# A conv, state-space and attention block on one Trainium2 core: one product moved to GpSimd, MLP and SiLU steps re-placed in a hand-made schedule

## What is computed

```python
# layer 0, per sample; xn = rmsnorm over channels of x
u, z = in_proj(xn);  u = silu(causal_conv4(u))           # forward; the same on the reversed sequence
B, C, dt = x_proj(u); delta = softplus(dt_proj(dt))
h = exp(delta*A)*h + (delta*u)*B;  y = sum_n h*C + u*D    # 16 states n, two directions d
g = (fwd + bwd) out-projected, y gated by silu(z)
local = sigmoid(depthwise3x3(xn) + dw_b) * xn             # the "local product"
x = x + res_scale * (g*scale_mod + local)
# layer 1, per sample: tokens t, 6 heads of 64, causal
t = t + attention(layernorm(t));  t = t + mlp(layernorm(t))   # mlp: narrow input of 32, 1536 hidden, gelu
```

## Time and profile before

| | us |
|---|---|
| median of 3 runs | 4040.74 (4040.47 to 4043.13) |
| profiled execution, its own time | 4045.01 |
| span of the profiled execution | 4043.1 |
| DVE busy | 3526.4 (87%) |
| PE busy | 3405.5 (84%) |
| POOL busy | 2820.7 (70%) |
| ACT busy | 2593.5 (64%) |

### The profile page before, as it was taken

How to read it: one execution, slowest core, us unless ns; L and a number is a source line. 1 busy time by engine, 2 the same in 40 slices (tenths; PEclk the granted TensorE clock), 3 DMA queues, 4 the chain that set the end, 5 groups by cost and what they waited for, 6 DMA issues and landing times.

```text
span 4043.1 us, 39821 instructions
## 1 busy us (share of the span) xinstructions
PE 3405.5 (84%) x11722; PEld 1723.8 (43%) x11722; DVE 3526.4 (87%) x2678; ACT 2593.5 (64%) x3592; POOL 2820.7 (70%) x1714
## 2 busy tenths in 40 slices
PE   7504499989999898988899889988989889985999
PEld 2101136623474245723366234742457233651473
DVE  6999999999999999999999999999999999999121
ACT  4533567676686767756676756867677666766363
POOL 3889886687866877677866878668776778668000
PEclk8757699988999899988999889988999889997999
DMA  3999897898977998788987989788987889789000
GB/s 103 234 248 240 190 242 181 207 209 207 219 190 188 227 214 202 190 201 198 237 188 199 222 202 216 186 193 224 215 198 194 203 201 232 179 197 221 6 7 16
DMA packets 220548, 770.79 MB, mean 191 GB/s; under 512 B 24908, under 2 KB 40574, under 8 KB 220062
## 3 DMA queue, kind: packets, MB, share of 16 engines
q0 software_dynamic: 113616, 413.71, 52.9%
q1 hardware_dynamic: 106702, 354.32, 26.4%
HBM read 339.60 MB, written 39.85 MB: 94 GB/s over the span
## 4 chain that ended last, share of the span: by engine, by line
PE 43%; DVE 21%; issue 12%; ACT 9%; POOL 8%; DMA 7%; ACTq 0%; DVEq 0%; POOLq 0%
DVE pB L1313 14%; PE pW L710 9%; PE pW L623 9%; DMA y<-hb 6%; PE pW L511 6%; POOL hb L1527 5%; PE pW L588 3%; PE pW L639 3%; PE pW L554 3%; ACT pt L1071 2%; POOL prob L1501 2%; PE pW L785 2%; DVE hb L1322 1%; PE pW L602 1%; PE pW L742 1%
## 5 line engine op out<-in xcount | busy, mean ns | idle before, releaser
L1313 DVE TENSOR_TENSOR_SCAN pB<-pB,hb 128x1024 f32<-128x1024 f32 x768 | 1757.4, 2288 | 64.1 <-ACT pB L889 52.1
L1542 POOL DMA_DIRECT2D y<-hb x765 | 748.9, 979 | 628.0 <-DVE hb L1322 578.3
L1527 POOL TENSOR_TENSOR hb<-du_f,b_row 128x1024 f32<-128x1024 f32 x384 | 1003.3, 2616 | 157.4 <-DMA y<-hb 71.9
L1527 POOL TENSOR_TENSOR hb<-uc_b,b_row 128x1024 f32<-128x1024 f32 x384 | 996.4, 2596 | 75.2 <-DMA y<-hb 62.0
L1322 DVE TENSOR_TENSOR hb<-pB,c_row 128x1024 f32<-128x1024 f32 x768 | 940.5, 1225 | 44.6 <-DVE pB L1313 0.5
L889 ACT ACTIVATE pB<-delta,vec 128x1024 f32<-128x1024 f32 x384 | 429.2, 1118 | 303.2 <-DVE hb L1322 290.3
L889 ACT ACTIVATE pB<-xres,vec 128x1024 f32<-128x1024 f32 x384 | 427.9, 1119 | 214.7 <-DVE hb L1322 213.7
L710 PE MATMUL pW<-area,pt 128*128 128x64 f32 x3456 | 440.1, 282 | 19.2 <-ACT pt L1071 11.5
L710 PEld LDWEIGHTS pW<-area,pt 128*128 128x128 f32 x3456 | 413.1, 196 | 68.9 <-ACT pt L1071 58.8
L1360 DVE TENSOR_REDUCE stat<-pW 128x1 f32<-128x640 f32 (+7 forms) x361 | 258.7, 753 | 162.4 <-PE pW L626 162.4
L530 PE MATMUL pW<-area,xn_area 128*128 128x512 f32 x576 | 260.7, 608 | 31.9 <-DVE area L1418 19.0
(11 more groups left out here) (185 smaller groups left out, 5010.3 us busy)
## 6 DMA issues: line engine op xcount, KB each, us to landing
y<-hb POOLq DMA_DIRECT2D x765, 512.0 KB, 7.7
b_row<-bc_rows SPq DMA_DIRECT2D x256, 512.0 KB, 5.9
c_row<-bc_rows SPq DMA_DIRECT2D x256, 512.0 KB, 5.8
du_f<-in_x SPq DMA_DIRECT2D x8, 1536.0 KB, 13.9
kept_residual<-in_x SPq DMA_DIRECT2D x8, 1536.0 KB, 18.9
xres<-kept_residual SPq DMA_DIRECT2D x8, 1536.0 KB, 14.5
out_x<-xa SPq DMA_DIRECT2D x7, 1536.0 KB, 9.5
kept_residual<-hb POOLq DMA_DIRECT2D x16, 512.0 KB, 5.3
```

Source lines behind the costliest of these rows:

```text
L1313: dve.tensor_tensor_scan(flow(d, buf), flow(d, buf), flow(d, hb[r % NHB][:, :]), 0.0, ALU.mult, ALU.add).then_inc(scan_done, 1)
L1527: pool.tensor_tensor(hb[r % NHB][:, :], du[d][:, k, :], b_row[g % 2][:, :], ALU.mult)\
L1542: pool.dma_start(y[:, k, :], hb[r % NHB][:, :], accum_op=ALU.add).then_inc(y_in[k], 16)
```

## The change

Five things change, in the order of the diff.

1. `mlp_add` moves from slot r+9 to r+10 of each half, and the second half starts at slot 81 instead of 82. `mlp_add` 0 moves from slot 81 to 82, where now also the second half's first GELU lies, behind it; its later GELUs move from 85, 87, 89 to 84, 86, 88; `mlp_out` 1 moves from 90 to 89; `mlp_add` 1 stays in 91.
2. `wo_add` 5 comes behind `next_norm` in slot 66. `next_square` goes from early to late in slot 63, so behind `decay(64)`. `step_silu` joins `SOON`: in slot 17 it now stands ahead of `proj` 2.
3. The local product of group 2 goes to GpSimd: ScalarE multiplies the sigmoid's result by `rs_col` in place (behind `skip`, ahead of slot 0), and GpSimd multiplies by `xnp` inside `keep_local`, which for this group is behind the input of slot 2.
4. At the head the order on ScalarE becomes: taps to 7, narrow copies, tap 8, sigmoid 0, `soft_abs` 0, sigmoid 2, sigmoid 1.
5. The narrow MLP input stays in PSUM (`pS`) from `mlp_scale` on: cast, split, low and fix read it there, and the 32-partition copy of `mlp_fix` (L1404) goes from VectorE to ScalarE.

```diff
-        ("mlp", c * (NFG + 1) + NFG, r + 2 * NFG), ("mlp_out", c, r + 2 * NFG), ("mlp_add", c, r + 2 * NFG + 1)]
+        ("mlp", c * (NFG + 1) + NFG, r + 2 * NFG), ("mlp_out", c, r + 2 * NFG), ("mlp_add", c, r + 2 * NFG + 2)]
...
-    + [("wo_add", t, S1 + (3 if t < 2 else 5)) for t in range(6)]
-    + [("next_square", 0, S1 + 2), ("next_mean", 0, S1 + 2), ("next_rstd", 0, S1 + 4), ("next_norm", 0, S1 + 5)]
+    + [("wo_add", t, S1 + (3 if t < 2 else 5)) for t in range(5)]
+    + [("next_square", 0, S1 + 2), ("next_mean", 0, S1 + 2), ("next_rstd", 0, S1 + 4), ("next_norm", 0, S1 + 5), ("wo_add", 5, S1 + 5)]
...
-       ("mlp_split", 0, S1 + 10), ("mlp_low", 0, S1 + 11), ("mlp_fix", 0, S1 + 11)] + mlp(0, S1 + 11) + mlp(1, S1 + 21), key=lambda x: x[2])
-SOON = [x for x in BEHIND if x[0] == "step_abs"]
+       ("mlp_split", 0, S1 + 10), ("mlp_low", 0, S1 + 11), ("mlp_fix", 0, S1 + 11)] + mlp(0, S1 + 11) + mlp(1, S1 + 20), key=lambda x: x[2])
+SOON = [x for x in BEHIND if x[0] in ("step_silu", "step_abs")]
...
                 if g == 2:
-                    pe.wait_ge(loc_ready, at(KT, b, BRANCH.index(1) + 1))
+                    pe.wait_ge(loc_ready, at(VK, b, VK))
...
-                    act.activation(taps[k], taps[k], ACT.Sigmoid).then_inc(sig_ready, 1)
+                    act.activation(taps[k], taps[k], ACT.Sigmoid).then_inc(sig_ready if k < VK else gate_ready, 1)
...
-                    act.copy(xr_a, xr_rest[:, :]).then_inc(xr_step, 1)
+                    act.copy(xr_a, pS).then_inc(xr_step, 1)
...
-                    act.copy(xr_b, xr_rest[:, :]).then_inc(xr_step, 1)
+                    act.copy(xr_b, pS).then_inc(xr_step, 1)
+                    act.copy(xr_a[3 * KI:4 * KI, :], pS[3 * KI:4 * KI, :]).then_inc(xr_step, 1)
...
-                elif kind == "next_square" and early:
+                elif kind == "next_square" and not early:
...
-                    tap_row_of(b, TAPS[6], 9)
+                    tap_row_of(b, TAPS[6], 8)
+                    narrow_copies(b, 0)
+                    tap_row_of(b, 8, 9)
                     gates(b, 0, 1)
-                    narrow_copies(b, 0)
-                    gates(b, 1, 2)
                     soft_abs(b, 0, 0)
-                    gates(b, 2, 3)
+                    gates(b, 1, 3)
...
+                    act.wait_ge(gate_ready, at(1, b, 1))
+                    act.activation(taps[VK], taps[VK], ACT.Identity, scale=rs_col).then_inc(gate_scaled, 1)
...
-                        dve.tensor_tensor(part, part, pW[:, c, :], ALU.mult).then_inc(xr_scaled, 1)
+                        dve.tensor_tensor(pW[:, c, :], part, pW[:, c, :], ALU.mult).then_inc(xr_scaled, 1)
...
-                    dve.tensor_tensor(xr_rest[:, :], xr_rest[:, :], xr_a, ALU.subtract).then_inc(xr_step, 1)
+                    dve.tensor_tensor(pS, pS, xr_a, ALU.subtract).then_inc(xr_step, 1)
...
-                    dve.tensor_copy(xr_a[3 * KI:4 * KI, :], xr_b[3 * KI:4 * KI, :]).then_inc(xr_step, 1)
-                    dve.tensor_tensor(xr_b[0:KI, :], xr_rest[0:KI, :], xr_b[0:KI, :], ALU.subtract)\
+                    dve.tensor_tensor(xr_b[0:KI, :], pS[0:KI, :], xr_b[0:KI, :], ALU.subtract)\
                        .then_inc(xr_step, 1)
...
-                    for k in BRANCH:
+                    for k in range(VK):
                         local(b, k)
...
-                pool.wait_ge(loc_ready, at(KT, b, BRANCH.index(k) + 1))
+                if k < VK:
+                    pool.wait_ge(loc_ready, at(VK, b, k + 1))
+                else:
+                    pool.wait_ge(gate_scaled, at(1, b, 1))
+                    pool.tensor_tensor(gate[k].rearrange("p (h w) -> p h w", w=WW),
+                                       gate[k].rearrange("p (h w) -> p h w", w=WW),
+                                       xnp[:, k, 1:1 + HH, 1:1 + WW], ALU.mult).then_inc(loc_last, 1)
+                    pool.wait_ge(loc_last, at(1, b, 1))
                 pool.dma_start(kept[b][128 * k:128 * k + 128, :], gate[k], accum_op=ALU.add).then_inc(kept_add[k], 16)
```

More of the change, by code:

```diff
@@ L237, in hybrid_block @@
         skip_added = sem("skip_added")
+        gate_ready, gate_scaled, loc_last = sem("gate_ready"), sem("gate_scaled"), sem("loc_last")
         da_ready, m1_done, scan_done, m2_done = (
@@ L1156, in iteration @@
                         act.preload_act_table_set(LOG_EXP)
-                        item("next_square", 0, -1, True)
+                        item("next_square", 0, -1, False)
                         prepare()
@@ L1278, in local @@
             def local(b, k):
-                dve.wait_ge(sig_ready, at(KT, b, BRANCH.index(k) + 1))
+                dve.wait_ge(sig_ready, at(VK, b, k + 1))
                 for i in range(KT):
@@ L1415, in item @@
                     dve.wait_ge(rstd_ready, at(1, b + 1, 1))
-                    dve.wait_ge(loc_ready, at(3, b + 1, 0))
+                    dve.wait_ge(loc_ready, at(VK, b + 1, 0))
+                    dve.wait_ge(loc_last, at(1, b + 1, 0))
                     for k in range(KT):
```

## The result

The changed kernel takes 4079.29 us (median of 4 runs, 4077.19 to 4082.35) against 4041.93 for the kernel before (4 runs): ratio 1.009, 95% interval 1.0078 to 1.0103. It is slower by 0.9%, some 37 us; +15 had been forecast. The profiled execution has a span of 4075.4 us, against 4043.1.

The account below looks back on a forecast made before the run. VectorE (87% busy, TensorE 84%) was taken as the bound in samples 0 to 7. Terms -22 - 12.8 + 19.6 + 0 + 35 - 10 + 5 = +15 us on the median 4040.7 gave 4056; range 4022 to 4074, the forecast's own 4046 to 4068.

Parts of the forecast that it names:

- wo_add 5 and the squares (no gain): Slots 63 to 71: moves remove VectorE waits of 1.91 and 1.82, but TensorE is no sooner; 0, bounds -3 and +6.
- SiLUs: Slots 16 to 22: proj 2 evacuated behind the SiLUs, proj 4 and scan 22 late, lower clock behind pauses; +35 us.
- Rival A: Projections don't gate slot 22, so the SiLU move gives its 0.9 instead of +35; sum -21, 4020; chance 0.17.
- Rival B: Clock stays up behind the new pauses: SiLU term +23, second half's hidden layer quicker; sum -6 to +3, 4040; chance 0.23.
- Rival C: TensorE moves along in slots 63 to 71, part of 22 us of waits is gain; about -3, 4038; chance 0.1.
- mlp_add 0 and the GELU in one slot: Second MLP half: decay 84 falls behind the first GELU and table load, scan 84 comes 2.8 us later; +19.6 us.
- mlp_add 1: End of second MLP half: a slot further behind its matmuls, its VectorE waits in 7 samples go; -12.8 us.
- Input in PSUM: MLP input: subtraction L1405 from 4.16 to 1.22 us, copy L1404 off VectorE, 2 us given back; net -22 us.
- rival D: GpSimd becomes the bound of slots 5 to 12, or L1405 stays at 4.16; +27 to +36, 4072; chance 0.1.
- Head: Head of each iteration: narrow copies ahead of tap 8 bring table, sigmoids and soft_abs sooner; mean 1.25 us, -10 in all.
- GpSimd's product: Early slots: product at 2.36 us delays the DMA and input queue behind it; 0.6 us per sample, +5 (0 to +12).

Follow-up runs that it names:

- p3: Kernel before with only wo_add 5 moved behind next_norm: 4065.14 us, +0.56% against before.
- e2: Changed kernel with wo_add 5 back ahead of next_square and next_norm, squares left late: 4058.63 us, +0.35% against before.
- c3: Changed kernel with step_silu late, wo_add 5 first, second half at S1 + 21, and group 2's product back on VectorE: 4002.3 us, -1.02% against before.
- c5: c3 with the squares early as well: 3995.59 us, -1.22% against before.
- e4: Changed kernel with the squares early again, wo_add 5 left behind next_norm: 4073.51 us, +0.66% against before.
- e1: Changed kernel with step_silu back behind the projections of its slot: 4039.53 us, -0.17% against before.
- p2: Kernel before with only step_silu moved ahead of the projections of its slot: 4081.75 us, +0.98% against before.
- e3: Changed kernel with the MLP's second half back one slot later (S1 + 21), mlp_add still two slots behind its matmuls: 4063.16 us, +0.41% against before.
- p1: Kernel before with only the MLP's narrow input in PSUM: 4019.09 us, -0.48% against before.
- c1: Changed kernel with step_silu late, wo_add 5 first and the second half at S1 + 21, all at once: 4004.21 us, -0.93% against before.
- p5: Kernel before with only mlp_add one slot later, the second half where it was: 4035.62 us, -0.19% against before.
- c4: c1 with the second half one slot later still (S1 + 22): 4018.81 us, -0.63% against before.

## Why the prediction was wrong

The direction and six of eight stretches were right; the change was +37 us where +15 was forecast, and 4079 lies above the forecast's own range (4046 to 4068) and the wide one (4022 to 4074). The step that failed is **wo_add 5 and the squares (no gain)**, "0, with bounds -3 and +6". The stretch measured +24.5, some 22 of it the change's; wo_add 5 alone (p3) is +20.6 there and +23 us timed, undone (e2) -21.2 and -22.

- *What the step said:* "the mean behind wo_add 5 starts about 1 us later, and this fills the 1.13 pause". It took VectorE's wait for the sixth `wo` as filled by the memsets and norms, so that `wo_add` 5 would come soon after TensorE's delivery. It never asked what `next_norm` itself waits for. Its first line waits for all six `wo`, so nothing moves into the pause, and 4.5 us of memsets and norms stand between the sixth `wo` and its add. TensorE idles 2.75 us and then pays 1.8 (4.54 less 2.74) at the lower clock; less the 1.13 us pause that this fills, 3.4. The chain of TensorE got 3.2 longer in b = 1. That TensorE's chain is tight here, and that waits would come up at `mlp_scale`, was read rightly, but the bound of +6 for all samples was drawn for a delay of 1 us. Late, the squares save up to 2 us a sample in slots 63 to 66 and it is given back in 66 to 71, as the step said (c3 against c5: 10.6 saved, 9.0 given back); whether they cost a little on top is open (e4, c5).
- *SiLUs:* forecast +35, measured +37.0; alone +34.7. The mechanism and the wait at scan 22 are as forecast (e1, p2), the cost of the pause too: 4.38 us for six products instead of 2.84. Rival A falls, since the projections gate slot 22; its sum was also short, for the 0.9 us won at slot 19 was counted once and not in each of 7 samples. Rival B falls, since the granted clock is 0.68 behind the pause (1039.0 to 1044.4) and 0.50 in the hidden layer. Rival C falls with slots 63 to 71, which grew.
- *mlp_add 0 and the GELU in one slot:* +19.6 forecast, +21.7 measured, with waits of 3.7 us in four samples and 5.4 in three where some 5 was forecast. Undone (e3) it gives 31.5 in its own slots and only 20 with those behind. *mlp_add 1:* -12.8 and -13.1, though `mlp_out` 1 comes one slot earlier and not the two that the prediction says.
- *Input in PSUM:* -22 and -24.5; 1.20 us for 1.22. Both halves of rival D fall, the slow subtraction and GpSimd as the bound of slots 5 to 12. The reason given, that the line no longer meets GpSimd's product over SBUF, is hardly tested by the line itself: in all 7 samples that product now starts 1.00 us into it and overlaps its last 0.2 us, where before it overlapped 2.65. What bears it out is L1326, also with one source in PSUM: 1223 to 1227 ns in all 768, some 280 of them beside a GpSimd product nearly all the way.
- *Head:* -10 forecast, -19.4 measured against the profiled execution, of which three heads were 1 to 3 us longer than the usual 40.4. Against p1, p2 and p3, with 284 to 284.8 us for seven heads, the change's 270.9 is -13 to -14. More than one thing shares it, and the prediction named one, the narrow copies. The product off VectorE is worth 6.7 by c1 and c3; with the product on VectorE the heads of c3 are 10.5 shorter than those of p5, whose tail is as early, which fits the narrow copies but wasn't measured by them alone. The place of the second half bears on it too: with it one slot later, e3 has heads 5.5 us longer than the change. How these add up to the 14 stays open.
- *GpSimd's product:* +5 forecast, +4.9 measured in slots 0 to 16, though each product takes 2.19 us and not 2.36. The other six runs that hold the product have 3.9 to 9.5 there, so that the queue behind it costs something was right, and that the size fits so closely is luck. By c1 and c3 the head gains as much as this costs.

By the timed runs the change is +36 (0.9% of 4042), and its parts alone are -19 (p1), +40 (p2) and +23 (p3). That leaves some -8 for the head, GpSimd's product and the two MLP slots together, of which only mlp_add's slot was run alone (p5).

## What to carry to other kernels

When an operation is to fill a wait, read the first wait of that operation too. If it is for the same producer, the order changes only who stands behind the pause, and there the one that feeds the next engine should be first. A gain in the tail of one iteration has to be followed into the next head: in p5 10.6 of 16.3 us came back there, along with a wait for a DMA that the slower tail had hidden, and in c4, against c1, more than all of it. And an evacuation that an in-order engine does behind a longer block can cost the matrix engine a pause and, behind it, its clock: here 2.90 us and another 1.5.

## What the runs showed of the hardware

Two pauses of TensorE of like length were followed by different clocks. In b = 1 after the change the six products behind a pause of 2.31 us (L786 at 866.02) took 2.76 us, as without a pause, at a granted clock of 1.00 in 866.0 to 868.8. Behind the pause of 2.14 us at 876.46 the hidden layer ran at 0.50, the lower level of 1.2 GHz, in both stretches read, 876 to 880 and 880 to 884, with each bf16 product at 0.60 us; those of the first half take 0.39. The kernel before does the same behind a pause of 1.62 (0.50 in 869 to 877).

```profile
860.64 0.39 PE L771 MATMUL pW<-pt,fc_bf 64*128 64x512 bf16 x1
...
866.02 2.76 PE L786 MATMUL pW<-du_f,pr_w 128*32 128x512 f32 x6 [2.31 <-ACT du_f L1125]
...
883.47 0.61 PE L771 MATMUL pW<-pt,fc_bf 64*128 64x512 bf16 x1
```

In slots 66 and 67 the pause of 2.75 us cost 1.8 more behind it, and the granted clock was 1.00 again in 815 to 820. GpSimd's product with a windowed source takes 2190 to 2201 ns in all 8 samples, less than the 2.35 of the plain product right ahead of the first one.
